# The maxima's rows issued by ScalarE, and the last sequence's values in two bursts

## The reference

```python
xn = _layernorm(x, axis=-1)
# attention
q = (x @ Wq.T + bq).reshape(b, s, h, hd).transpose(0, 2, 1, 3)   # k, v alike
scores = jnp.einsum('bhqd,bhkd->bhqk', q, k) / math.sqrt(hd)
scores = jnp.where(causal, scores, -jnp.inf)
attn = jax.nn.softmax(scores, axis=-1)
out = jnp.einsum('bhqk,bhkd->bhqd', attn, v)
out = out.transpose(0, 2, 1, 3).reshape(b, s, d) @ Wo.T + bo
# experts
logits = jnp.einsum('btd,ed->bte', x, gate_w)
top_val, top_idx = jax.lax.top_k(logits, 2)
top_w = jax.nn.softmax(top_val, axis=-1)
y_all = jnp.einsum('btd,edm->btem', x, We)
out = jnp.sum(jnp.take_along_axis(y_all, top_idx[..., None], axis=2) * top_w[..., None], axis=2)
```

## Time and profile before

| | |
|---|---|
| median of 3 runs | 518.96 us |
| lowest and highest run | 516.93 and 520.93 us |
| the profiled execution | 520.78 us, span 518.6 us |
| granted TensorE clock, mean | 0.99 of full |
| transfers of the maxima's rows | 64, of 8 KB |

### The profile page before, as it was taken

How to read it: one execution, slowest core, us unless ns; L and a number is a source line. 1 busy time by engine, 2 the same in 40 slices (tenths; PEclk the granted TensorE clock), 3 DMA queues, 4 the chain that set the end, 5 groups by cost and what they waited for, 6 DMA issues and landing times.

```text
span 518.6 us, 17312 instructions
## 1 busy us (share of the span) xinstructions
PE 481.6 (93%) x6274; PEld 395.7 (76%) x6274; DVE 420.5 (81%) x1111; ACT 397.5 (77%) x1062; POOL 346.0 (67%) x561
## 2 busy tenths in 40 slices
PE   2549799999999999999999999999999999999994
PEld 1427688888887888888888888878787888888762
DVE  5897688888888888888888898888888898887711
ACT  3645678878887888788888888878887888887763
POOL 7265647777777677777777777767767678754443
PEclk9999989999999999999999999999999999999997
DMA  4755746655547456655465566654646566650000
GB/s 125 197 130 123 188 100 158 153 134 144 143 121 159 121 151 158 152 140 142 114 166 134 142 148 149 159 149 112 162 120 152 126 153 152 149 140 13 15 13 21
DMA packets 64281, 67.79 MB, mean 131 GB/s; under 512 B 6828, under 2 KB 59180, under 8 KB 59484
## 3 DMA queue, kind: packets, MB, share of 16 engines
q1 hardware_dynamic: 64196, 66.68, 52.0%
HBM read 44.90 MB, written 21.23 MB: 128 GB/s over the span
## 4 chain that ended last, share of the span: by engine, by line
PE 77%; DMA 7%; ACT 6%; DVE 4%; issue 3%; SPq 1%; POOL 0%; DVEq 0%; ACTq 0%; POOLq 0%
PE m L841 19%; PE oT_ps L911 15%; PE scoreT_ps L887 10%; PE score_ps L867 10%; DMA qstack<-mT 6%; PE scoreT_ps L892 6%; PE score_ps L861 5%; PE m L1000 3%; PE m L953 3%; ACT upper L549 2%; PE m L1018 2%; ACT probs L499 2%; PE m L926 2%; PE m L1025 1%; PE m L962 1%
## 5 line engine op out<-in xcount | busy, mean ns | idle before, releaser
L625 DVE TENSOR_REDUCE negmax<-score_ps 128x2 f32<-128x512 f32 (+1 forms) x384 | 250.1, 678 | 52.3 <-PE score_ps L867 51.9
L499 ACT ACTIVATE probs<-scoreT_ps 128x512 f32<-128x512 f32 x384 | 216.8, 603 | 78.9 <-PE scoreT_ps L892 41.8
L394 POOL TENSOR_TENSOR fours<-lower,upper 128x512 f32<-128x512 f32 x64 | 81.7, 1277 | 61.4 <-ACT upper L549 61.4
L841 PE MATMUL m<-we_hl,xnT_hl 128*128 128x512 f32 x384 | 114.4, 420 | 0.0
L867 PE MATMUL score_ps<-kstack,qstack 72*128 72x128 bf16 (+1 forms) x1024 | 104.4, 224 | 5.6 <-DVE negmax L625 5.5
L887 PE MATMUL scoreT_ps<-qstack,kstack 123*128 123x128 bf16 (+1 forms) x1024 | 101.8, 221 | 7.6 <-DMA qstack<-mT 5.7
L911 PE MATMUL oT_ps<-probs,vaug 128*32 128x256 f32 (+1 forms) x2048 | 97.7, 331 | 1.3 <-ACT probs L499 1.2
L887 PEld LDWEIGHTS scoreT_ps<-qstack,kstack 123*128 123x128 bf16 (+1 forms) x1024 | 70.0, 98 | 21.6 <-issue 16.5
L911 PEld LDWEIGHTS oT_ps<-probs,vaug 128*32 128x32 f32 x2048 | 57.6, 110 | 30.7 <-ACT probs L499 1.9
L549 ACT ACTIVATE upper<-m,weight 128x128 f32<-128x128 f32 x256 | 73.3, 376 | 9.3 <-PE m L841 9.3
L867 PEld LDWEIGHTS score_ps<-kstack,qstack 72*128 72x128 bf16 (+1 forms) x1024 | 72.5, 100 | 8.4 <-DVE negmax L625 7.8
(11 more groups left out here) (81 smaller groups left out, 651.1 us busy)
## 6 DMA issues: line engine op xcount, KB each, us to landing
kstack<-scratch SPq DMA_DIRECT2D x93, 192.0 KB
scratch<-parts SPq DMA_DIRECT2D x64, 192.0 KB, 2.4
qstack<-scratch SPq DMA_DIRECT2D x62, 192.0 KB
qstack<-scratch SPq DMA_DIRECT2D x31, 256.0 KB
x_sb<-in_x SPq DMA_DIRECT2D x32, 128.0 KB, 2.3
scratch<-parts SPq DMA_DIRECT2D x32, 128.0 KB, 1.9
out<-out_sb SPq DMA_DIRECT2D x32, 128.0 KB, 3.3
qstack<-mT SPq DMA_DIRECT2D x64, 8.0 KB, 2.1
```

What stands on the lines that cost most here:

```text
L394: g.tensor_tensor(fours[:, :, q, :], lower[:, :, q, :], upper[:, :, q, :], ALU.add).then_inc(pool_sum, 1)
L499: a.activation(o, i, ACT.Exp, scale=SCALE).then_inc(act_exp, 1)
L625: v.tensor_reduce(o, score_ps[n % 2][:].rearrange("p (h k) -> p h k", h=w), axis=AX.X, op=ALU.max, negate=True).then_inc(dve_max, 1)
L841: ins = tn.matmul(o, l, r, start=first, stop=l is low)
```

## The change

The wait for `dve_mT` and the two transfers into `qstack` leave SP's slot, where they stood between the output's store and the load of x, and stand in ScalarE's slot at n = 2, ahead of `part1`. The buffers, the semaphores and their counts are the same. On PE the values of the last sequence are treated as those of the others: groups 0 and 1 at n = 3 of slot 33, groups 2 and 3 at n = 6.

```diff
@@ SP
             def slot(t, s):
                 if has(s, -3):
                     store(t + (-3))
-                if has(s, -1):
-                    m = t + (-1)
-
-                    sp.wait_ge(dve_mT, upto(m))
-                    for part in range(MAX_PARTS):
-                        sp.dma_start(qstack[m.buf][MAX_ROW + part:MAX_ROW + part + 1], mT[:, part]).then_inc(dma_max, 16)
                 if s == 1:
@@ ScalarE
                         a.copy(mT[:, 0], m0[0:H, 0:S]).then_inc(act_mT, 1)
+                    if n == 2 and has(s, -1):
+                        act.wait_ge(dve_mT, upto(mix))
+                        for part in range(MAX_PARTS):
+                            act.dma_start(qstack[mix.buf][MAX_ROW + part:MAX_ROW + part + 1], mT[:, part]).then_inc(dma_max, 16)
                     if n == 2 and has(s, PRE):
                         part1(t + PRE)
@@ PE
-                    if s == NSEQ and n in (9, 11):
-                        values(mix, (9, 11).index(n))
-                    if s == NSEQ + 1 and n in (2, 4):
-                        values(fin, (2, 4).index(n) + 2)
-                    if n == 3 and has(s, -2) and s <= NSEQ:
+                    if n == 3 and has(s, -2):
                         values(fin, 0)
                         values(fin, 1)
@@ PE
-                    if n == 6 and has(s, -2) and s <= NSEQ:
+                    if n == 6 and has(s, -2):
                         values(fin, 2)
                         values(fin, 3)
```

## The result

| | before | after |
|---|---|---|
| median | 518.81 us (4 runs, 516.93 to 520.93) | 525.96 us (4 runs, 524.76 to 526.26) |
| profiled execution | 520.78 us, span 518.6 | 524.76 us, span 522.6 |

The ratio is 1.0118, 95% interval 1.0084 to 1.0151: the changed kernel is slower, by 7.1 us between the medians and by 4.4 to 7.8 us by the interval (6.1 at its ratio). The forecast was 4.7 us. The two profiled executions stand only 4.0 us apart: the one of before took more than its median, the one of after was the fastest of its four. The medians give the size, the profiles the places.

The account below looks back on a forecast made before the run. PE's own work, 14.40 us per slot, was taken as the bound. PE's wait +11.9, stretched issues +1.0, short waits -3.1, third sequence -3.8, tail -1.3: +4.7 on 518.96, so 523.7 us, range 517 to 530.

Parts of the forecast that it names:

- The lead of `rest` and the loop: Slots 3 to 29: part 1 1.19 us late against 0.77 us lead, PE waits 0.44 us per slot, +11.9 us.
- The stretched issues: Transfer pairs on ScalarE sometimes take longer than 1.15 us, as on SP: 0 to 2.1 us, taken as +1.0.
- The short waits: PE's eight short waits for the maxima's rows shrink, as PE arrives 0.44 us later: -3.1 us.
- The third sequence: Slot at 54.50 to 73.54: rows from ScalarE's queue pass the stack loads, PE keeps its clock: -3.8 us.
- my own list of what SP loses: SP loses one wait and two issues; only the x load stands right behind, going 2.5 us earlier: put at nothing.
- the second rival: Third sequence's slot: maxima's rows don't pass the stack loads, so the 3.8 us gain is missing: 527.5 us, chance 0.21.
- The tail: Last sequence's values in the last slot: group 3 at 508.66 and not 509.97, -1.3 us.
- the rival in which they fit the lead: ScalarE's pair costs under 0.72 us, so PE hardly waits for `rest`: -4.0 us, 515 us, chance 0.16.
- the one in which they wait for it: ScalarE's issue starts only after its running exponential, PE waits 0.63 us per slot: +10.3, 529.3 us, chance 0.18.

Follow-up runs that it names:

- the two parts alone: Kernel before with one half of the change each: ScalarE's transfers only, ratio 1.0128, 6.6 us; last sequence's values in two bursts only, ratio 0.9971, 1.1 us.

## Why the prediction was right, and where it wasn't

**The lead of `rest` and the loop.** Right, and shown from both sides: moved behind part 1 the wait is gone, with a third issue it grows by the issue. Measured 0.36 us per slot (14.76) where I had 0.44: counted from the first issue to part 1, PE doesn't wait up to 0.92 us, and my numbers made that 0.84 (from 250.10 to 250.94, that is 0.75 after part 1's 250.19). 27 slots: +9.7 in place of +11.9.

**The stretched issues.** The mechanism was right, the term too small: +3.6 in place of +1.0. Halving the row for want of knowledge was one error, taking one execution for the rule the other: over 1.15 us the pairs stood 2.1 us in all in the kernel before, but 3.3 to 5.5 in four other profiles in which SP issued them, and 3.3 to 3.8 in three in which ScalarE did. In all eight the pair of slot 16 is stretched, in seven that of slot 7, whichever engine issues; why is open.

**The short waits.** PE arrived later and most of them went, but two waits of 0.86 and 0.68 us came, behind landings of 4.22 and 4.05 us (the median is 2.3), longer than any but slot 2's before. Beside the stretched issues, what slots 3 to 29 took over their plain periods went from 3.7 us to 2.0 (404.12 - 27 x 14.76 - 3.6): -1.7 in place of -3.1. The 3.7 was itself one execution's: in four profiles whose middle slots are those of before it is 3.7, 2.9, 1.2 and 3.3. What delays single landings is open.

**The third sequence.** The size was right (19.04 to 15.08, -4.0; I had -3.8), the step was wrong, so that the size was luck. "From ScalarE the rows are in another queue. If they pass the loads" fails: from ScalarE's queue they landed when they had landed from SP's, at 62.8 us. What I had overlooked is in my own list of what SP loses: "nothing but the x load stands right behind it there" holds for all slots but the first, where `load_stacks` of the third sequence stands behind the wait (line 319). By my steps the second rival (the rows don't pass, 527.5 us) should have come true, and by its own condition it did; the loads going sooner took its price away.

**The tail.** -1.5 us by the order of work, where I had -1.3. The tail of the profiled pair is 2.7 us shorter; the other 1.2 go with the clock, and not with the bursts, as said.

**In sum:** 9.7 + 3.6 - 1.7 - 4.0 - 1.5 = +6.1, against +4.7 predicted and 4.4 to 7.8 measured (7.1 between the medians); the two parts alone add up to 6.6 - 1.1 = +5.5. The forecast came near as errors went both ways: the wait taken 2.2 too dear, the stretched issues 2.6 and the short waits 1.4 too favourably. The issues on ScalarE were as predicted: a pair of 1.17 us, which rules out the rival in which they fit the lead, and a start while the exponential runs, which rules out the one in which they wait for it.

## What to carry to other kernels

An engine that issues a transfer pays for the issue in its own stream, about 0.6 us here, and whoever waits for the next instruction on it pays too; put issues behind the last instruction that another engine is waiting for, not ahead of it. Before moving a wait out of a queue, list what stands behind it in every iteration, the odd ones at the start and end too: here it held back six loads of 1.2 MB in a single slot. And a small urgent transfer wasn't saved by its own queue while the DMA engines were busy with large ones; sending the large ones sooner did it.

## What the runs showed of the hardware

Not expected: with the stack loads going out late, the maxima's rows landed between 62.8 and 63.2 us whichever queue they came from, in four kernels with second issues at 55.75 to 57.16. An issue on ScalarE starts while its computing part works (at 295.29, with the exponential until 295.47; in the kernel with the issues behind part 1 the second at 258.72, with part 1 until 259.08, and the first, which stands behind part 1 in the program, at 258.18, ahead of part 1's start at 258.25). And issues are stretched on either engine, five pairs of 32 on SP before and seven on ScalarE after, by 0.1 to 1 us.
